# Query and key pieces of a head pair side by side in the attention operands: half as many operand transfers, each twice as large, and the row of maxima sent in two transfers

## The chip, the cores and the metric

The kernel runs on one core of one Trainium2 chip. The metric is the device time of one execution in microseconds (us); lower is better. The timeline positions used below are microseconds from the start of the profiled span.

## The reference, cut to what matters

Two sequences of 512 tokens with 128 features pass through four conditioned layers: a gated recurrent layer with ternary weights, a transformer block with 16 heads (no mask), a masked block of MLPs, and a causal transformer block with 16 heads. The change touches only the two attentions. For layer 3 the reference is

```
qkv = (x @ Wqkv).reshape(b, t, 3, H, hd).transpose(2, 0, 3, 1, 4)
scores = einsum('bhqd,bhkd->bhqk', q, k) * hd ** -0.5
scores = where(causal, scores, -inf)
attn = softmax(scores, axis=-1)
out = einsum('bhqk,bhkd->bhqd', attn, v)
```

with H = 16 heads of hd = 8 features. Layer 1 does the same without the causal mask.

## The kernel before, in words

**Operands.** Queries and keys are fp32 values that are split into three bf16 pieces each (high, middle, low; `spl`, held in the tile `tern`). A score is the sum of six products of pieces, so a head needs 8 features times 6 pieces; with a row of zeros and a row that carries the softmax maximum this makes 8 rows a feature and 64 rows a head. Two heads (a pair) stand above each other in the 128 partitions. These operands are the "stacks", in the tile `big`: partition 8i + place holds one piece of feature i, and along the row lie, for attention a, first all queries and then all keys: `p (a k b r t)`, with k = query or key, b = batch, r = head pair (8 of them), t = token (512). `stack_of` (L79) cuts out a head. `PIECES` and `PIECES_K` say which query and which key piece meet in each of the six products, `PLACE` at which of the 8 rows the product stands.

**Stack transfers.** The pieces are computed in feature layout and have to be spread to every eighth partition by DMA. The SP queue does this in L317 to L325: for each attention, for each batch b, for each part (high, middle, low, made by ScalarE at L1157, ScalarE at L1161 and VectorE at L835), for queries and then keys, it waits until that part of that operand is made and issues the transfers that need it. Each is 128 KB: 128 runs of 1 KB, from 128 partitions to 16 (`stacks[PLACE[j]::8, a, qk, b]`). There are 12 for each batch of each attention, 48 in all. TensorE waits for the 12 of batch 0 at L1488, before the first score product of the attention, and for those of batch 1 at L1460, half way through. The order of issue in batch 0 is three query transfers when the high query piece is there, three key transfers, two and two for the middle pieces, one and one for the low ones.

**Maxima.** A unit u is four heads of one batch; an attention has 8 units. In a unit TensorE computes the scores with queries as rows (L1469, in ring slots handed out by `schedule`, L243), VectorE takes the negated maximum over the keys (L961) into `nm`, GpSimd splits the 16 columns of `nm` into three bf16 parts (`max_parts`, L432 to L443, into `nm3`), TensorE turns `nm3` (L1437), VectorE copies the result to `nmp` (L966: 64 partitions by 128), and SP sends it (L326 to L331) in one transfer of 16 KB, 64 runs of 256 bytes, from 64 partitions into 8 partitions of `big`, the rows `MAX_PLACE` of the query stacks of the two head pairs of the unit. Then TensorE computes the scores a second time, now with keys as rows and the maximum inside the product (L1506); it waits for the maxima's row at L1501, once a unit. ScalarE takes the exponential (L1192), and TensorE multiplies by the values (L1483). All instructions of an engine run in the order in which they are written; TensorE's order is written out at L1510 to L1531.

**Fill.** Early on, three transfers (L313 to L315) put zeros and ones into the remaining rows of `big` from an array in DRAM, `in_fill`: one to 16 partitions at a step of 8 and two to 8 partitions at a step of 16, each with 64 KB for every partition.

Of the kernel before, what the change touches and what calls it, by code (L numbers as in the profile page):

```python
# [57 lines left out]
def build(nc, x_in, out, wa_in, w0_in, w1_in, w2_in, w3_in, row0_in, rowa_in, rowg_in, col_in, mask_in, c_in, ident_in,  # L58
          cmask_in, inv_in, sel_in, fill_in):
    with ExitStack() as ctx:  # L60
# [16 lines left out]
        stacks = big[:, :].rearrange("p (a k b r t) -> p a k b r t", a=2, k=2, b=B, r=NP)  # L77

        def stack_of(a, qk, b, h, lo, hi):  # L79

            row = 64 * (h % 2)
            return stacks[row:row + 64, a, qk, b, h // 2, lo:hi]
# [81 lines left out]
        spl = tern[:, 0:6 * B * S].rearrange("p (k i b t) -> p k i b t", k=2, i=3, b=B)  # L164
        resid = tern[:, 6 * B * S:6 * B * S + 4 * S].bitcast(F32).rearrange("p (k t) -> p k t", k=2)
# [4 lines left out]
        nm3 = sb("nm3", [128, 2, 2, MPARTS, 8], BF16)  # L170
# [115 lines left out]
        def _(sp):  # L286
# [30 lines left out]
            for a, (layer, causal) in enumerate(((1, False), (3, True))):  # L317

                for b in range(B):
                    for part, made in enumerate(("hi", "mid", "split")):  # L320
                        for qk, pieces in enumerate((PIECES, PIECES_K)):
                            sp.wait_ge(sem(f"a{a}_{made}"), 2 * b + qk + 1)
                            for j in [j for j, piece in enumerate(pieces) if piece == part]:
                                sp.dma_start(stacks[PLACE[j]::8, a, qk, b], spl[:, qk, part, b, :]).then_inc(  # L324
                                    sem(f"a{a}_stack{b}"), 16)  # L325
                for u in range(2 * TB):  # L326
                    b, g = u // 4, u % 4

                    sp.wait_ge(sem(f"a{a}_nmp"), u + 1)
                    sp.dma_start(stacks[MAX_PLACE::16, a, 0, b, 2 * g:2 * g + 2], nmp[:, u % 2]).then_inc(  # L330
                        sem(f"a{a}_mrow{u % 2}"), 16)  # L331
# [7 lines left out]
        def _(pool):  # L339
# [76 lines left out]
            for n, kind, layer in SEQ:  # L416
# [11 lines left out]
                if kind == "att":  # L428
# [3 lines left out]
                    def max_parts(u):  # L432

                        m = nm[:, u % 2].rearrange("p (k r) -> p k r", k=2)
                        pool.wait_ge(sem(f"a{a}_max"), n_max * (u + 1))
                        part = [nm3[:, u % 2, :, i] for i in range(3)]
                        left = nmr[:].rearrange("p (k r) -> p k r", k=2)
                        link(nc.gpsimd.tensor_copy(part[0], m))  # L438
                        link(nc.gpsimd.tensor_tensor(left, m, part[0], ALU.subtract))
                        link(nc.gpsimd.tensor_copy(part[1], left))  # L440
                        nc.gpsimd.tensor_tensor(part[2], left, part[1],
                                                ALU.subtract).then_inc(sem(f"a{a}_nm3"), 1)
                        pool.wait_ge(sem(f"a{a}_nm3"), u + 1)  # L443
# [38 lines left out]
        def _(dve):  # L482
# [443 lines left out]
            for n, kind, layer in SEQ:  # L926
                if kind == "att":
# [6 lines left out]
                    for item, u, *step_ in (x for slot in schedule(len(steps)) for x in slot):  # L934
# [20 lines left out]
                        if item == "max":  # L955
# [3 lines left out]
                            first = 8 * (hs[0] % 2) + TB * (hs[0] // 2) + qt  # L959
                            dst = nm[:, u % 2, first:first + TB * (len(hs) - 1) + 1:TB]  # L960
                            v.tensor_reduce(dst, src[:, 0:w * len(hs)].rearrange("p (h w) -> p h w", w=w),  # L961
                                            AX.X, ALU.max, negate=True).then_inc(sem(f"a{a}_max"), 1)
                        elif item == "parts":
                            if u >= 2:
                                dve.wait_ge(sem(f"a{a}_mrow{u % 2}"), 16 * (u // 2))
# [246 lines left out]
        def _(pe):  # L1212
# [185 lines left out]
            for n, kind, layer in SEQ:  # L1398
                if kind == "att":
# [22 lines left out]
                    def ring_item(item, u, i=0):  # L1422
# [33 lines left out]
                        else:  # L1456
                            qt, hs, wd = steps[i]
                            if u == 4 and i == 0:
                                pe.wait_ge(sem(f"a{a}_split"), 4)
                                pe.wait_ge(sem(f"a{a}_stack1"), 16 * 2 * len(PIECES))  # L1460
# [27 lines left out]
                    pe.wait_ge(sem(f"a{a}_stack0"), 16 * 2 * len(PIECES))  # L1488
# [6 lines left out]
                    def scores(s):  # L1495
# [4 lines left out]
                        if kt == 0 and p == 0:  # L1500
                            pe.wait_ge(sem(f"a{a}_mrow{u % 2}"), 16 * (u // 2 + 1))  # L1501
# [121 lines left out]
```

## Time and profile before

| | us |
|---|---|
| median of 3 runs (lowest to highest) | 458.74 (458.56 to 458.84) |
| the profiled execution | 458.03 |
| its span (first to last instruction) | 456.3 |
| TensorE matmul busy in the span | 303.2 (66%) |
| VectorE busy | 307.5 (67%) |
| ScalarE busy | 240.1 (53%) |
| GpSimd busy | 133.7 (29%) |
| DMA queue of SP, share of the 16 DMA engines | 13.7% |
| attention of layer 1, first to last maximum and score | about 174 to 283 |
| attention of layer 3 | about 336 to 434 |

1.7 us of the execution lie outside the span. Engines work beside each other, so busy times don't add up; what sets the time is the chain of work that ended last, followed back from release to release. In the rows below, "idle before <-X" in square brackets is the time for which the engine had nothing to do and what ended it; SPq is the instruction queue of the SP engine, which issues the DMAs; PEld is TensorE's load of the stationary operand. The granted TensorE clock is 1.00 for 2.4 GHz and 0.50 for 1.2 GHz.

### The profile page before, as it was taken

The numbers are of one execution on the slowest core, as the hardware profiler recorded it, in microseconds if no ns is written. First come the engines' busy times: TensorE is split into PE (matmuls) and PEld (weight loads), VectorE is DVE, ScalarE is ACT, GpSimd is POOL, SyncE is SP. The second block draws the span as 40 slices with busy tenths as digits, with TensorE's granted clock in tenths as the row PEclk, the third lists the DMA queues.
The fourth block names the chain that finished last, engine by engine and source line by source line (L and its number), as shares of the span: only waits on it lengthen the run. The fifth ranks groups of instructions, "written<-read, shape, count | busy, mean of one in ns | idle before, by whom it ended". The sixth has DMA issues, their size and how long they took to land.

```text
span 456.3 us, 5838 instructions
## 1 busy us (share of the span) xinstructions
PE 303.2 (66%) x1953; PEld 148.0 (32%) x1954; DVE 307.5 (67%) x791; ACT 240.1 (53%) x422; POOL 133.7 (29%) x237
## 2 busy tenths in 40 slices
PE   0012862642055647699999987885777899889686
PEld 0001821431022432122222222554443444344254
DVE  0688788776858865999999950433568678766330
ACT  2276926555166421267777777433342456665742
POOL 0013102232236240253223004218340344444520
PEclk9999985555555576679999999999796599999999
DMA  7960044000000033200000000000037000000001
GB/s 240 414 260 0 1 92 94 0 0 0 0 1 1 0 96 102 79 5 1 3 3 2 3 2 1 0 1 0 0 84 195 3 5 2 3 3 5 2 0 46
DMA packets 12138, 19.96 MB, mean 44 GB/s; under 512 B 2598, under 2 KB 11050, under 8 KB 11434
## 3 DMA queue, kind: packets, MB, share of 16 engines
q1 hardware_dynamic: 12108, 19.59, 13.7%
q8 instruction: 15, 0.25, 0.2%
q14 instruction: 15, 0.12, 0.1%
HBM read 12.51 MB, written 0.52 MB: 29 GB/s over the span
## 4 chain that ended last, share of the span: by engine, by line
PE 38%; DVE 30%; ACT 11%; POOL 7%; issue 6%; DMA 3%; SPq 2%; DVEq 0%; ACTq 0%; POOLq 0%
DVE nm L961 10%; PE ps L1483 8%; PE ps L1469 6%; PE pe L1395 4%; PE ps L1551 4%; PE pe L1506 3%; POOL rstd L344 2%; PE ps L1442 2%; ACT scr L1079 2%; DMA big<-nmp 2%; DVE st L539 2%; SPq L324 1%; DMA big<-in_wa 1%; DVE xn L549 1%; PE ps L1266 1%
## 5 line engine op out<-in xcount | busy, mean ns | idle before, releaser
L961 DVE TENSOR_REDUCE nm<-ps 128x1 f32<-128x512 f32 (+2 forms) x224 | 131.8, 647 | 21.6 <-PE ps L1469 20.4
L1192 ACT ACTIVATE scr<-pe 128x1024 f32<-128x1024 f32 (+3 forms) x128 | 105.6, 867 | 66.0 <-PE pe L1506 65.0
L1469 PE MATMUL ps<-big 64*128 64x512 bf16 (+3 forms) x256 | 71.4, 381 | 6.9 <-DVE nm L961 4.5
L1483 PE MATMUL ps<-scr 128*32 128x512 f32 (+3 forms) x512 | 58.8, 531 | 6.3 <-ACT scr L1167 4.8
L344 POOL TENSOR_TENSOR rstd<-var,half 128x4 f32<-128x4 f32 x26 | 28.5, 1097 | 102.7 <-DVE var L544 77.2
L1506 PE MATMUL pe<-big 64*128 64x512 bf16 (+3 forms) x256 | 44.0, 355 | 3.4 <-ACT scr L1192 2.0
L1469 PEld LDWEIGHTS ps<-big 64*128 64x128 bf16 x256 | 21.0, 101 | 54.1 <-DVE nm L961 44.3
L450 POOL TENSOR_SCALAR_AFFINE_SELECT scr<-scr 128x256 f32<-128x256 f32 x64 | 25.8, 407 | 37.7 <-ACT scr L1192 36.4
L438 POOL CAST nm<-nm 128x16 bf16<-128x16 f32 x16 | 3.1, 196 | 87.2 <-DVE nm L961 87.2
L1466 PE MATMUL ps<-cmask 64*128 64x128 bf16 (+1 forms) x192 | 25.7, 261 | 3.3 <-DMA big<-tern 2.8
L549 DVE TENSOR_SCALAR xn<-x_tok,mv,rstd 128x128 f32<-128x128 f32 x60 | 17.1, 348 | 15.8 <-POOL rstd L344 15.8
L1395 PE MATMUL pe<-hT,w 128*128 128x512 f32 x48 | 24.5, 635 | 3.5 <-ACT hT L1146 3.5
L1205 ACT ACTIVATE scr<-pe,col 128x512 f32<-128x512 f32 x24 | 16.3, 688 | 14.5 <-PE pe L1395 14.5
L1506 PEld LDWEIGHTS pe<-big 64*128 64x128 bf16 x256 | 12.8, 94 | 33.6 <-ACT scr L1192 18.8
L990 DVE TENSOR_TENSOR x_tok<-x_tok,ps 128x512 f32<-128x512 f32 x6 | 4.1, 687 | 21.3 <-PE ps L1551 21.2
L1071 ACT ACTIVATE junk<-scr 128x128 f32<-128x128 f32 x24 | 7.1, 297 | 21.0 <-DVE scr L672 20.9
L1266 PE MATMUL pe<-ident,xn 128*128 128x128 f32 x20 | 4.4, 358 | 20.6 <-ACT xn L1079 13.0
L1483 PEld LDWEIGHTS ps<-scr 128*32 128x32 f32 x512 | 10.4, 108 | 21.4 <-issue 10.2
L1079 ACT ACTIVATE scr<-scr,magic,q 128x128 f32<-128x128 f32 x32 | 12.7, 480 | 8.2 <-DVE q L693 8.2
L1146 ACT ACTIVATE hT<-ps,modc 128x512 f32<-128x512 f32 x8 | 6.2, 776 | 20.3 <-PE ps L1266 20.3
L1266 PE MATMUL ps<-ident,scr 128*128 128x128 f32 x24 | 6.4, 431 | 15.2 <-ACT scr L1079 14.4
L976 DVE RECIPROCAL rec<-ps 128x16 f32<-128x16 f32 x16 | 4.0, 252 | 18.5 <-PE ps L1442 18.5
(222 smaller groups left out, 584.1 us busy)
## 6 DMA issues: line engine op xcount, KB each, us to landing
big<-tern SPq DMA_DIRECT2D x48, 128.0 KB, 2.4
big<-in_wa SPq DMA_DIRECT2D x1, 2304.0 KB, 12.7
w<-in_w SPq DMA_DIRECT2D x2, 1152.0 KB, 19.5
big<-in_wa SPq DMA_DIRECT2D x1, 1344.0 KB, 6.4
big<-in_w SPq DMA_DIRECT2D x1, 1024.0 KB, 14.6
w<-in_w SPq DMA_DIRECT2D x1, 896.0 KB, 20.2
rowg<-in_rowg SPq DMA_DIRECT2D x1, 832.0 KB, 18.6
row<-in_row SPq DMA_DIRECT2D x1, 640.0 KB, 14.8
```

Of the source, the lines that this page charges most:

```text
L344: nc.gpsimd.tensor_tensor(dst, src, half[0:src.shape[0], 0:n], ALU.pow).then_inc(sem(done), 1)
L450: nc.gpsimd.affine_select(block_, block_, [[0, 2], [1, 128]], ALU.is_ge, 0.0, base=0, channel_multiplier=-1).then_inc(sem(f"a{a}_low"), 1)
L549: last = v.tensor_scalar(xn[:, t], x_tok[:, t], mv[:, t, 0:1], rstd[:, t:t + 1], ALU.subtract, ALU.mult)
L961: v.tensor_reduce(dst, src[:, 0:w * len(hs)].rearrange("p (h w) -> p h w", w=w), AX.X, ALU.max, negate=True).then_inc(sem(f"a{a}_max"), 1)
L1079: last = s_.activation(dst[:, t], src[:, t], ACT.Identity, bias=magic[:, 0:1], scale=q4[:, 3, m, t:t + 1])
L1192: s_.activation(P[:, kt % 2, 2 * p:2 * p + 2, q0:S], E[(e - 1) % 2][:, :, q0:S], ACT.Exp, scale=SCALE).then_inc(sem(f"a{a}_p"), 1)
L1395: t_.matmul(bank[2 + i % 4], m["w"][:, m["at"] + c * D:m["at"] + (c + 1) * D], hT[:, b], start=True, stop=True).then_inc(sem(f"n{n}_h"), 1)
L1466: t_.matmul(diagonal, cmask[row:row + 64, m], above.broadcast_to([64, len(hs), 128]), start=(m == 0), stop=False, skip_group_check=True)
L1469: last = t_.matmul(dst[:, k * wd:(k + 1) * wd], stack_of(a, 0, b, HG * g + h, qt * 128, (qt + 1) * 128), stack_of(a, 1, b, HG * g + h, 0, ...
L1483: last = t_.matmul(bank[6][32 * h:32 * h + 32, q0:S], V[b][:, kt, HG * g + h, :], P[:, kt % 2, h, q0:S], start=(kt == 0), stop=(kt == TB - 1),
L1506: last = t_.matmul(E[s % 2][:, j, q0:S], stack_of(a, 1, b, h, kt * 128, (kt + 1) * 128), stack_of(a, 0, b, h, q0, S), start=True, stop=True)
L1551: last = t_.matmul(bank[6 + b][:, i * D:(i + 1) * D], hid[:, b, c, i * D:(i + 1) * D], gated_w(n, b, c), start=(c == 0), stop=(c == m["n"] ...
```

## The change

In the stacks the query and the key of a head pair now lie side by side: `p (a b r k t)`. For one product j, the query piece and the key piece go to the same 16 partitions, and in them to neighbouring rows of 512 tokens, so one transfer of 256 KB carries both. Its source has for each of 128 partitions two runs of 1 KB that are a fixed step apart. It can be issued when the later of the two pieces is made, for both operands: the SP queue now waits for query and key together (`2 * b + 2`). Of the six transfers of a batch, one (j = 0) goes out after the high pieces, three (j = 1, 3, 4) after the middle pieces, two (j = 2, 5) after the low ones. TensorE's waits count 6 transfers in place of 12. The query rows of the two head pairs of a unit no longer lie next to each other, so the maxima's row is sent in two transfers of 8 KB, from 32 partitions each, and the waits for it count 32 in place of 16; `nm` and `nm3` are ordered by head pair first to fit. The filling array has its ones where the keys now lie.

```diff
@@ -74,12 +74,12 @@
 
         big = sb("big", [128, 2 * NH * B * S], BF16)
         QK_N = NP * B * S
-        stacks = big[:, :].rearrange("p (a k b r t) -> p a k b r t", a=2, k=2, b=B, r=NP)
+        stacks = big[:, :].rearrange("p (a b r k t) -> p a b r k t", a=2, k=2, b=B, r=NP)
 
         def stack_of(a, qk, b, h, lo, hi):
 
             row = 64 * (h % 2)
-            return stacks[row:row + 64, a, qk, b, h // 2, lo:hi]
+            return stacks[row:row + 64, a, b, h // 2, qk, lo:hi]
         wf32 = big[:, :].bitcast(F32)
         NWA, NW0 = sum(WA_N), sum(W0_N)
         wa_f = wf32[:, 0:NWA]
@@ -162,12 +162,13 @@
 
 
         spl = tern[:, 0:6 * B * S].rearrange("p (k i b t) -> p k i b t", k=2, i=3, b=B)
+        spl_ = tern[:, 0:6 * B * S].rearrange("p (k b t) -> p k b t", k=6, b=B)
         resid = tern[:, 6 * B * S:6 * B * S + 4 * S].bitcast(F32).rearrange("p (k t) -> p k t", k=2)
         V = [scr[:, 4096 + 2048 * b:6144 + 2048 * b].rearrange("p (t h e) -> p t h e", t=TB, h=NH) for b in range(B)]
         P = scr[:, 0:2 * HG * S].rearrange("p (i h t) -> p i h t", i=2, h=HG)
         hid = scr[:, 0:4 * 2 * S].rearrange("p (b c t) -> p b c t", b=B, c=4)
         nm = sb("nm", [128, 2, 16])
-        nm3 = sb("nm3", [128, 2, 2, MPARTS, 8], BF16)
+        nm3 = sb("nm3", [128, 2, 4, MPARTS, 4], BF16)
         nmr = sb("nmr", [128, 16])
         nmp = sb("nmp", [64, 2, 128], BF16)
         oT = scr[:, 8192:9216].rearrange("p (k t) -> p k t", k=2)
@@ -318,17 +319,18 @@
 
                 for b in range(B):
                     for part, made in enumerate(("hi", "mid", "split")):
-                        for qk, pieces in enumerate((PIECES, PIECES_K)):
-                            sp.wait_ge(sem(f"a{a}_{made}"), 2 * b + qk + 1)
-                            for j in [j for j, piece in enumerate(pieces) if piece == part]:
-                                sp.dma_start(stacks[PLACE[j]::8, a, qk, b], spl[:, qk, part, b, :]).then_inc(
-                                    sem(f"a{a}_stack{b}"), 16)
+                        sp.wait_ge(sem(f"a{a}_{made}"), 2 * b + 2)
+                        for j in [j for j in range(6) if max(PIECES[j], PIECES_K[j]) == part]:
+                            q_piece, k_piece = PIECES[j], 3 + PIECES_K[j]
+                            both = spl_[:, q_piece:k_piece + 1:k_piece - q_piece, b]
+                            sp.dma_start(stacks[PLACE[j]::8, a, b], both).then_inc(sem(f"a{a}_stack{b}"), 16)
                 for u in range(2 * TB):
                     b, g = u // 4, u % 4
 
                     sp.wait_ge(sem(f"a{a}_nmp"), u + 1)
-                    sp.dma_start(stacks[MAX_PLACE::16, a, 0, b, 2 * g:2 * g + 2], nmp[:, u % 2]).then_inc(
-                        sem(f"a{a}_mrow{u % 2}"), 16)
+                    for pair in range(2):
+                        sp.dma_start(stacks[MAX_PLACE::16, a, b, 2 * g + pair, 0],
+                                     nmp[32 * pair:32 * pair + 32, u % 2]).then_inc(sem(f"a{a}_mrow{u % 2}"), 16)
             for b in range(B):
                 sp.wait_ge(sem("x_done"), b + 1)
                 sp.dma_start(out[b].rearrange("(t p) d -> p t d", p=128), x_tok[:, bt(b)]).then_inc(sem("stored"), 16)
@@ -431,10 +433,10 @@
 
                     def max_parts(u):
 
-                        m = nm[:, u % 2].rearrange("p (k r) -> p k r", k=2)
+                        m = nm[:, u % 2].rearrange("p (k r) -> p k r", k=4)
                         pool.wait_ge(sem(f"a{a}_max"), n_max * (u + 1))
                         part = [nm3[:, u % 2, :, i] for i in range(3)]
-                        left = nmr[:].rearrange("p (k r) -> p k r", k=2)
+                        left = nmr[:].rearrange("p (k r) -> p k r", k=4)
                         link(nc.gpsimd.tensor_copy(part[0], m))
                         link(nc.gpsimd.tensor_tensor(left, m, part[0], ALU.subtract))
                         link(nc.gpsimd.tensor_copy(part[1], left))
@@ -956,13 +958,13 @@
                             qt, hs, w = steps[step_[0]]
                             if u >= 2 and step_[0] == 0:
                                 dve.wait_ge(sem(f"a{a}_nm3"), u - 1)
-                            first = 8 * (hs[0] % 2) + TB * (hs[0] // 2) + qt
-                            dst = nm[:, u % 2, first:first + TB * (len(hs) - 1) + 1:TB]
+                            first = 8 * (hs[0] // 2) + TB * (hs[0] % 2) + qt
+                            dst = nm[:, u % 2, first:first + 8 * (len(hs) - 1) + 1:8]
                             v.tensor_reduce(dst, src[:, 0:w * len(hs)].rearrange("p (h w) -> p h w", w=w),
                                             AX.X, ALU.max, negate=True).then_inc(sem(f"a{a}_max"), 1)
                         elif item == "parts":
                             if u >= 2:
-                                dve.wait_ge(sem(f"a{a}_mrow{u % 2}"), 16 * (u // 2))
+                                dve.wait_ge(sem(f"a{a}_mrow{u % 2}"), 32 * (u // 2))
                             v.tensor_copy(nmp[:, u % 2], src.bitcast(BF16)[0:64, 0:128]).then_inc(sem(f"a{a}_nmp"), 1)
                         elif item == "proj":
                             dve.wait_ge(sem("n_bias"), B * n + u + 1)
@@ -1457,7 +1459,7 @@
                             qt, hs, wd = steps[i]
                             if u == 4 and i == 0:
                                 pe.wait_ge(sem(f"a{a}_split"), 4)
-                                pe.wait_ge(sem(f"a{a}_stack1"), 16 * 2 * len(PIECES))
+                                pe.wait_ge(sem(f"a{a}_stack1"), 16 * len(PIECES))
                             if causal:
                                 diagonal = dst[:, 0:wd * len(hs)].rearrange("p (h w) -> p h w", w=wd)[:, :, wd - 128:wd]
                                 row = 64 * (hs[0] % 2)
@@ -1485,7 +1487,7 @@
                                              tile_position=(0, 32 * h))
                         last.then_inc(sem(f"a{a}_pv"), 1)
 
-                    pe.wait_ge(sem(f"a{a}_stack0"), 16 * 2 * len(PIECES))
+                    pe.wait_ge(sem(f"a{a}_stack0"), 16 * len(PIECES))
                     pe.wait_ge(sem("filled"), 16 * 3)
                     pe.wait_ge(sem("n_var"), B * n + 2)
                     for x in slots[0]:
@@ -1498,7 +1500,7 @@
                         b, g = u // 4, u % 4
                         q0 = 128 * kt if causal else 0
                         if kt == 0 and p == 0:
-                            pe.wait_ge(sem(f"a{a}_mrow{u % 2}"), 16 * (u // 2 + 1))
+                            pe.wait_ge(sem(f"a{a}_mrow{u % 2}"), 32 * (u // 2 + 1))
                         if s >= 2:
                             pe.wait_ge(sem(f"a{a}_p"), s - 1)
                         for j in range(2):
@@ -1609,7 +1611,7 @@
         "col": np.stack(cols, 1), "mask": g["mask_BxS_bk0"].reshape(B * TB, 128).T, "c": g["cond_1024"],
         "ident": np.eye(128, dtype=np.float32), "cmask": cmask.astype(ml_dtypes.bfloat16),
         "inv": np.tile(np.array([1.0 / k for k in numel], np.float32), (128, 1)), "sel": sel,
-        "fill": np.stack([np.zeros(2 * NH * B * S), np.tile(np.repeat([0.0, 1.0], NP * B * S), 2)]).astype(ml_dtypes.bfloat16),
+        "fill": np.stack([np.zeros(2 * NH * B * S), np.tile(np.repeat([0.0, 1.0], S), 2 * NP * B)]).astype(ml_dtypes.bfloat16),
     }
     arrays = {k: np.ascontiguousarray(v) for k, v in arrays.items()}
     nc = bacc.Bacc("TRN2", target_bir_lowering=False, num_devices=1)
```

## Rows read from the trace of the kernel before

**Rows 1.** The page, chain that ended last: share of the span by line

```profile
DVE nm L961 10%; PE ps L1483 8%; PE ps L1469 6%; PE pe L1395 4%; PE ps L1551 4%; PE pe L1506 3%; POOL rstd L344 2%; PE ps L1442 2%; ACT scr L1079 2%; DMA big<-nmp 2%; DVE st L539 2%; SPq L324 1%; DMA big<-in_wa 1%; DVE xn L549 1%; PE ps L1266 1%
```

**Rows 2.** Chain in order of time, around 340: start us, us, what

```profile
336.37 0.55 SPq L324
...
343.42 2.37 DMA big<-tern
...
345.83 0.62 PE ps L1466 x4
```

**Rows 3.** Timeline of layer 3's start: start, us, engine, line, op, tiles, [idle before]

```profile
338.19 1.22 ACT L1161 CAST tern<-tern 128x512 bf16<-128x512 f32 x2 [0.99 <-DVE tern L831]
338.84 1.29 DVE L835 TENSOR_TENSOR tern<-tern 128x512 bf16<-128x512 f32 x2
...
345.83 0.14 PEld L1466 LDWEIGHTS ps<-cmask 64*128 64x128 bf16 x4 [3.01 <-DMA big<-tern]
...
345.95 0.68 DVE L847 COPY scr<-pe 128x512 f32<-128x512 f32 x1
...
346.69 5.97 DVE L961 TENSOR_REDUCE nm<-ps 128x2 f32<-128x256 f32 x11
```

**Rows 4.** Lines L324 and L330: issue time ns (min/median/max), and landing

```profile
L324 SPq DMA_DIRECT2D big<-tern x48: 531/600/615, 164.4 to 351.2; - x48
...
DMA to landing us min/median/max: 2.3/2.4/2.6
...
L330 SPq DMA_DIRECT2D big<-nmp x16: 579/590/629, 193.4 to 419.7; - x16
```

**Rows 5.** Windows: stretch, length, five engines' busy us, PEclk, DMA share, GB/s

```profile
65.00:69.80 4.80, 2.04 (x4) 0.37 (x2) 4.63 (x9) 3.74 (x19) 1.00 (x1) 0.59 1.01 218
69.80:74.70 4.90, 0.36 (x2) 0.40 (x3) 3.79 (x11) 3.54 (x8) 1.75 (x2) 0.50 0.50 107
...
11.00:16.00 5.00, 0.56 (x2) 0.50 (x2) 1.81 (x10) 2.08 (x6) 0.00 (x0) 1.00 0.98 419
337.60:345.40 7.80, 3.53 (x16) 2.15 (x16) 5.10 (x9) 4.34 (x8) 1.27 (x1) 1.00 0.74 202
```

**Rows 6.** Timeline of layer 1's start

```profile
166.28 0.62 ACT L1161 CAST tern<-tern 128x512 bf16<-128x512 f32 x1 [0.24 <-DVE tern L831]
...
174.24 0.10 PEld L1469 LDWEIGHTS ps<-big 64*128 64x128 bf16 x1 [0.33 <-DMA big<-tern]
...
174.35 0.78 ACT L1146 ACTIVATE hT<-pe,modc 128x512 f32<-128x512 f32 x1 [7.46 <-PE pe L1266]
```

**Rows 7.** Timeline and chain: issue of maxima's rows, and the scores that wait for them

```profile
193.36 0.61 SPq L330 DMA_DIRECT2D big<-nmp  x1
...
195.35 1.36 PE L1506 MATMUL pe<-big 64*128 64x512 bf16 x4
...
355.09 0.63 SPq L330 DMA_DIRECT2D big<-nmp  x1
...
357.04 0.65 PE L1506 MATMUL pe<-big 64*128 64x512 bf16 x2
...
203.29 0.61 SPq L330 DMA_DIRECT2D big<-nmp  x1
...
205.67 0.10 PEld L1506 LDWEIGHTS pe<-big 64*128 64x128 bf16 x2
...
213.69 0.58 SPq L330 DMA_DIRECT2D big<-nmp  x1
...
216.67 0.10 PEld L1506 LDWEIGHTS pe<-big 64*128 64x128 bf16 x2
...
235.69 3.61 DMA big<-nmp
```

**Rows 8.** Windows of the low clock in layer 3, and TensorE's timeline at its end

```profile
345.80:362.80 17.00, 15.65 (x97) 7.57 (x97) 14.08 (x27) 4.57 (x6) 2.68 (x11) 0.50 0.32 89
...
360.95 1.93 PE L1483 MATMUL ps<-scr 128*32 128x512 f32 x8
```

## The prediction, made before any run of the changed kernel

> **What bounds the kernel now.** I read the chain that ended last first. No engine owns it: the maxima on VectorE have a tenth of the span, the products with the values 8%, and of what the change touches only two small entries appear, the stack issues on SP's queue (1%) and the maxima's transfers (2%) [rows 1]. So the change can act at few places. Next the chain in order of time. At layer 3's start it runs along SP's queue: the first stack transfer is issued at 336.37, the twelfth at 343.42, 0.64 us apart, and TensorE starts 2.4 us after the last, at 345.83 [rows 2]. The timeline shows TensorE idle for 3.0 us there, ended by the transfer; but VectorE, which must take the first maximum next, is busy with other work until 346.63 and starts at 346.69 [rows 3]. So the stacks are late for TensorE, and only just in time for VectorE: earlier stacks gain little, later ones cost in full. At layer 1's start TensorE waits 0.33 us only [rows 6]. Last, the maxima's rows: 16 issues of 0.59 us, a time that a stack issue of eight times the bytes has too [rows 4].
>
> **The transfers: what an issue and 256 KB take.** An issue takes 0.60 us whether it carries 64 runs or 128 [rows 4], so I take 0.64 from issue to issue for the new ones too; the upper bound is double, one issue that takes the time of the two it replaces, 1.29 us. What the bytes take is the question. The stack stream now moves 202 GB/s with the DMA engines busy for 0.74 of the time [rows 5]: filled up, that would be 202 / 0.74 = 273 GB/s and 0.96 us for 256 KB. Nearer is the fill of the very same partitions (16 at a step of 8), which keeps all 16 engines busy (share 1.01) and still moves 218 GB/s, and with 8 partitions on half the engines 107; loads to all 128 partitions reach 419 at the same share [rows 5]. I read this as the destination being the limit: engines that write to these 16 partitions get in each other's way. Then 256 KB take 262144 B / 218 GB/s = 1.2 us. The bounds are 0.64 (issue alone) and 1.29. I take 1.2, since it is the saturated row with the same destination, and back-to-back transfers of 256 KB with 0.64 between issues will saturate.
>
> The Trainium skill has two rules that pull apart here. "DMA: Bandwidth & Descriptors", in its rules for kernel authors, says to coalesce many small transfers into a large one; by its line of bytes over 436 GB/s, 256 KB would take 0.6 us (an estimate from that page), and the sum would be that of the fast rival below. "SBUF — State Buffer", in the section on the DMA port swizzle, says that a partition's port is set by bits 2 to 4 and bit 6 of its number, by which 16 partitions at a step of 8 reach only half of the 16 ports. The fill's 218 against 419 GB/s sides with the second.
>
> **Layer 3, batch 0.** Before, half of the transfers (the query pieces and first key pieces) went out from 336.37 on, while later pieces were being made. Now five of six wait for the middle key piece, ready at 338.19 + 1.22 = 339.41 [rows 3]; the first is long through by then. The low pieces are there at 338.84 + 1.29 = 340.13 [rows 3] and are not late, since three transfers stand before them. The fixed part of a transfer is 2.4 - 0.64 = 1.75 us [rows 4]. So the last lands at 339.45 + 1.75 + 5 x 1.2 = 347.2, against 345.8: TensorE starts 1.4 us later, VectorE with it: **+1.4**. Bounds: with 0.64 it lands at 344.4, 1.4 earlier, of which VectorE, free at 345.95 + 0.68 = 346.63 only, would pass on little, so -1.4 is the end and -0.1 the likely value there; with 1.29, 347.65, +1.9. Batch 1's six transfers queue behind and end about 354.5, before the first maxima's row of this attention is issued at 355.09 [rows 7], which is itself pushed back: 0.
>
> **Layer 1, batch 0.** The middle key piece is ready at 166.28 + 0.62 = 166.90 [rows 6]: 166.95 + 1.75 + 6.0 = 174.7. Before, twelve issues from 164.4 on gave 164.4 + 11 x 0.64 + 2.4 = 173.9 [rows 4]. TensorE comes to the wait at about 174.2, makes one maximum's scores in 0.6 us and then needs the modulated input of batch 1, ready at 174.35 + 0.78 = 175.13 [rows 6]: **+0.1**, bounds 0 and +0.6. Batch 1 is not wanted for a long time: 0.
>
> **The maxima's rows.** The second transfer of each unit is issued 0.64 us after the first, so the row is complete up to 0.64 us later; its bytes are nothing. VectorE's copy waits only for the row two units back. Who waits is TensorE at L1501, and behind it every later score and ring item. The unit's time from issue to scores tells the slack, since a row lands within 1.95 us (355.09 to 357.04 [rows 7]). The first units of both attentions have 1.99 and 1.95 us [rows 7]: nothing to spare beyond what hides behind running matmuls; **+0.4** and **+0.5** (each 0 to 0.65). The second unit has 2.38 [rows 7], in both attentions: **+0.1** each at most, 0.1 together. The later ones have 2.98 as in 213.69 to 216.67 [rows 7], which covers 1.95 + 0.64: 0. That holds for nine of the twelve remaining units; in the other three the transfer itself was slow, as the 3.61 at 235.69 [rows 7], and TensorE waited for it. A transfer issued 0.64 us later on the same stalled engine probably ends with the first: **+0.2** for the three, bounds 0 and 1.9.
>
> **The rest.** GpSimd's four small operations and VectorE's maxima write the same number of elements at another step; the fill moves the same bytes; neither is timed otherwise: 0. SP issues 24 fewer stack transfers and 16 more maxima's transfers, and nobody waits for its queue elsewhere.
>
> **The clock.** TensorE runs at 1.2 GHz from about 345.8 to 362.8 in layer 3, and at the end of that stretch the chain is TensorE's: eight value products take 1.93 us there [rows 8]. If the rise stays at its place, the 1.9 us of work that is pushed past it runs at twice the speed: up to -0.95. I take **-0.7**. If the rise moves with the work or beyond it, nothing is given back and more is lost.
>
> **Sum.** 1.4 + 0.1 + 0.4 + 0.5 + 0.1 + 0.2 - 0.7 = +2.0 us. On the profiled execution that is 458.03 + 2.0 = 460.0; the median of the runs, 458.74, is 0.7 above it, so I forecast **460.7** for the median.
>
> **Rivals.**
> (a) *The port limit is milder* (0.96 us for 256 KB, the engines' own rate): the stacks land at 346.0, +0.2, and the sum is 0.2 + 1.2 - 0.4 = +1.0 or less; with a first-unit delay that hides behind VectorE, +0.6: 459.4. For it: the stream's 0.74 share. Against: the fill. Chance 0.22.
> (b) *Faster*: transfers are paced by issue alone (0.64). The stacks are there at 344.4, before the clock falls, between 345.4 [rows 5] and 345.8 [rows 8]. Then TensorE has work earlier and the clock can stay up in the 17 us [rows 8]. From 357.04 [rows 7] to 362.8 the chain is mostly TensorE's, 5.8 us at the low clock, half of it at the other: -0.1 - 2.9 + 1.0 (maxima's rows, a little cheaper so) = -2.0, 456.7. It decides at the stacks' landing: before about 345. For it: the wait of 3.0 us is real. Against: the fill's rate. Chance 0.12.
> (c) *The clock rises later*: the late start leaves one stretch emptier, the low clock lasts some 3 us longer, and instead of -0.7 it costs about +1.5: 462.9. Chance 0.2.
> (d) *An issue of 256 runs takes twice as long* (1.29): five issues end the chain at 339.45 + 4 x 1.29 + 2.4 = 347.0 or a little more, nearly my number by another cause: 460.7. It would show in the issue rows. Chance 0.05.
> My forecast has the remaining 0.41.
>
> **How the numbers follow.** A measurement of this kernel tells a change of 0.2% (0.9 us) from none. Faster by more than that is (b), with a part of (a)'s low end: 0.13. Within: most of (a) and the low end of the forecast: 0.24. Slower: 0.63. The range takes in (a), (c) and the bounds of the maxima's rows, and leaves out (b) and the largest sums: 458.0 to 463.3.
>
> **What would show it.** In the changed profile the stack transfers should have issues of about 0.6 us but land, the last of batch 0, 4 to 5 us after issue instead of 2.4; a window over them should show about 215 GB/s with a DMA share near 1; TensorE's wait at layer 3's start should grow from 3.0 to about 4.4 us and VectorE's first maximum come 1.3 us later against its L847 copy. The maxima's row should show two issues 0.64 us apart and a wait of TensorE at the first unit of each attention, and none in the third. I am wrong if the landing stays at 2.4 to 3 us, or if the stacks arrive before 345.8.

## The result and the profile after

The changed kernel took **465.84 us** (median of 4 runs, 465.80 to 466.63) against 458.78 for the kernel before (4 runs beside it): a ratio of 1.0136 with an interval of 1.0094 to 1.0178, 7.06 us more. I forecast 460.7 with a range of 458.0 to 463.3: slower was right, the size was not. Run again on another chip (after_again) it stood at 1.0113 (1.0087 to 1.0139), 5.2 us more at 460, with the kernel before between 458.65 and 461.63 in 15 executions. The two intervals overlap; I take 5.2 us, which rests on more executions, for the change's average. The profile below is one execution, and its 7.8 us also depend on where the steps of TensorE's clock fell in it.

| | before | after |
|---|---|---|
| profiled execution, us | 458.03 | 465.80 |
| span, us | 456.3 | 464.0 |
| matmul busy, us | 303.2 | 309.6 |
| VectorE busy, us | 307.5 | 307.5 |
| DMA queue of SP, share of 16 engines | 13.7% | 15.2% |

VectorE did the same work in the same time; matmuls took 6.4 us more with the same count of 1953. The page after, chain that ended last, answers to [rows 1]:

```profile
PE 38%; DVE 31%; ACT 10%; POOL 8%; issue 6%; DMA 5%; SPq 2%; DVEq 0%; POOLq 0%; ACTq 0%
DVE nm L963 12%; PE ps L1485 8%; PE ps L1471 5%; PE ps L1553 4%; PE pe L1397 4%; DMA big<-tern 3%; PE pe L1508 3%; POOL rstd L346 2%; PE ps L1444 2%; ACT scr L1081 2%; DVE st L541 2%; PE ps L1268 1%; DVE xn L551 1%; DMA big<-in_wa 1%; PE pe L1234 1%
...
big<-tern SPq DMA_DIRECT2D x24, 256.0 KB, 4.8
```

The stack transfers are now 3% of the chain by themselves, and their median from issue to landing is 4.8 us where it was 2.4 [rows 4]. The chain in order of time at layer 3's start, which answers to [rows 2]:

```profile
343.98 0.60 SPq L326
344.62 0.61 SPq L326
345.27 0.62 SPq L326
345.94 0.62 SPq L326
346.60 5.92 DMA big<-tern
352.57 0.62 PE ps L1468 x4
```

Issues are still 0.6 us, but the last transfer lands 5.9 us after its issue, because those ahead of it are still moving. A window over the stream (columns as in [rows 5]):

```profile
345.50:352.00 6.50, 3.73 (x11) 2.15 (x9) 3.07 (x5) 3.40 (x5) 0.00 (x0) 0.74 1.11 216
```

216 GB/s with a DMA share above 1: the engines are full, at the rate of the fill, 218 GB/s [rows 5], and not at that of a load to all partitions.

From the products that make queries and keys (339.14 in the timeline after, 334.60 before) to TensorE's start on the stacks it is 13.43 us, before 11.23: 2.2 us more. In layer 1 the stacks land at 175.17, 1.2 us later than before. TensorE then makes the products of batch 1 at 1.2 GHz:

```profile
175.21 0.60 PE L1471 MATMUL ps<-big 64*128 64x512 bf16 x1 [1.07 <-DMA big<-tern]
175.75 2.07 PE L1362 MATMUL ps<-hT,w 128*128 128x512 f32 x2
177.75 0.61 PE L1471 MATMUL ps<-big 64*128 64x512 bf16 x2
178.29 2.07 PE L1362 MATMUL pe<-hT,w 128*128 128x512 f32 x2
```

The second pair (the key product) took 1.48 us before, at 2.4 GHz from 178.5 on; now 2.07, since the clock rises at 181.6 only. The copy of unit 0's maxima, 193.12 before, starts at 194.85. Then the maxima's row of that unit, in the chain of the changed kernel (answers to [rows 7]):

```profile
194.93 0.14 DVE nmp L968
195.07 0.02 issue
195.08 0.65 SPq L332
195.73 0.04 issue
195.77 2.21 DMA big<-nmp
197.99 0.14 issue
198.12 0.58 PE pe L1508
```

3.04 us from issue to scores against 1.99 [rows 7]. A larger item stands behind it. Windows of the changed kernel, then of the kernel before, over 198.9 to 205.5:

```profile
198.90:205.50 6.60, 6.24 (x28) 1.33 (x24) 4.51 (x8) 4.15 (x5) 1.86 (x5) 0.50 0.01 2
205.50:212.10 6.60, 6.13 (x43) 1.43 (x42) 6.26 (x12) 5.26 (x6) 2.38 (x4) 1.00 0.01 2
```

```profile
198.90:205.50 6.60, 6.16 (x45) 1.38 (x42) 6.19 (x12) 5.35 (x6) 4.23 (x8) 1.00 0.01 2
```

For 6.6 us TensorE is at 1.2 GHz where it was at 2.4, and gets 28 matmuls done in place of 45. From the first exponential of unit 0 to that of unit 1 it is 11.55 us against 9.99. Whether the change moved this rise, or only this execution has it there, the two profiles can't tell; the experiments come back to it.

### The profile page after: what moved, and what is told of

Its sections match the earlier page's. It is cut to its first block, busy times and chain, and to the rows that moved or that the text cites. A ratio compares the mean times of both kernels' runs of the same rounds, so it can differ in the third digit from the quotient of the medians.

```text
span 464.0 us, 5830 instructions
## 1 busy us (share of the span) xinstructions
PE 309.6 (67%) x1953; PEld 150.6 (32%) x1954; DVE 307.5 (66%) x791; ACT 240.2 (52%) x422; POOL 133.8 (29%) x237
## 3 DMA queue, kind: packets, MB, share of 16 engines
q1 hardware_dynamic: 11852, 19.59, 15.2%
## 4 chain that ended last, share of the span: by engine, by line
PE 38%; DVE 31%; ACT 10%; POOL 8%; issue 6%; DMA 5%; SPq 2%; DVEq 0%; POOLq 0%; ACTq 0%
DVE nm L963 12%; PE ps L1485 8%; PE ps L1471 5%; PE ps L1553 4%; PE pe L1397 4%; DMA big<-tern 3%; PE pe L1508 3%; POOL rstd L346 2%; PE ps L1444 2%; ACT scr L1081 2%; DVE st L541 2%; PE ps L1268 1%; DVE xn L551 1%; DMA big<-in_wa 1%; PE pe L1234 1%
## 5 line engine op out<-in xcount | busy, mean ns | idle before, releaser
L1485 PE MATMUL ps<-scr 128*32 128x512 f32 (+3 forms) x512 | 59.8, 539 | 6.3 <-ACT scr L1169 4.8
L1397 PE MATMUL pe<-hT,w 128*128 128x512 f32 x48 | 24.8, 641 | 3.5 <-ACT hT L1148 3.5
L1207 ACT ACTIVATE scr<-pe,col 128x512 f32<-128x512 f32 x24 | 16.3, 688 | 15.2 <-PE pe L1397 15.2
```

The source lines that it names most:

```text
L1397: t_.matmul(bank[2 + i % 4], m["w"][:, m["at"] + c * D:m["at"] + (c + 1) * D], hT[:, b], start=True, stop=True).then_inc(sem(f"n{n}_h"), 1)
L1485: last = t_.matmul(bank[6][32 * h:32 * h + 32, q0:S], V[b][:, kt, HG * g + h, :], P[:, kt % 2, h, q0:S], start=(kt == 0), stop=(kt == TB - 1),
```

## The experiments

Two theories stood against each other first: the stacks' lateness with the clock (1), or the second maxima transfer (2); and whether the lateness comes from deferral or from the size of the transfers (3). The clock's steps fall at other places in each execution, so a profile shows a delay directly, and the ratios, from many executions, the average.

### Two maxima transfers alone (maxrow_two)

```diff
-                    sp.dma_start(stacks[MAX_PLACE::16, a, 0, b, 2 * g:2 * g + 2], nmp[:, u % 2]).then_inc(
-                        sem(f"a{a}_mrow{u % 2}"), 16)
+                    for pair in range(2):
+                        sp.dma_start(stacks[MAX_PLACE::16, a, 0, b, 2 * g + pair],
+                                     nmp[32 * pair:32 * pair + 32, u % 2]).then_inc(sem(f"a{a}_mrow{u % 2}"), 16)
...
```

Left out of the cut are the order of `nm` and `nm3` and the waits for 32, as in the change.

> The kernel before, with only the maxima's row sent in two transfers (and nm, nm3 ordered by head pair); stacks as before. Theory 1 (the stacks' lateness is the cause, the clock's rise doubles it): the scores of the first unit of each attention come 0.5 to 0.7 us later, the other units not at all; without a moved clock step that is +1.0 to +1.3 us, 459.8 to 460.0; if the clock's rise in layer 1 moves too, one step of about 3.4 us later costs up to 1.6 more. Theory 2 (the second maxima transfer is the main cost): most of the 7 us is here, 464 or more.

Ratio 1.0057 (1.0032 to 1.0082), 2.6 us (1.5 to 3.8): twice my price, and half of the change's average. The profile bears out the places: from unit 0's copy to the first exponential it is 0.70 us longer in layer 1 (3.90 against 3.20) and 0.56 in layer 3 (3.44 against 2.88). In its chain the second issue follows at once, and its transfer lands 2.20 us behind it:

```profile
194.19 0.64 SPq L331
194.84 0.04 issue
194.88 2.20 DMA big<-nmp
197.08 0.14 issue
197.22 1.01 PE pe L1507 x3
```

The other 1.3 us of the 2.6 aren't in these two waits, and where they lie on average stays open. In this profile unit 0 to unit 1 takes 11.55 us, with the clock low until 203.8, as in the changed kernel. Layer 3 loses another 1.5 us: its first maximum comes 13.59 us behind the products that make queries and keys (12.09 before), though the stacks are as early (11.34 and 11.23). The products of batch 1 fell into a low stretch there:

```profile
343.68 2.04 PE L1361 MATMUL ps<-hT,w 128*128 128x512 f32 x2 [1.87 <-ACT hT L1147]
```

The same pair took 1.13 us in the kernel before. early_halves, below, has the two maxima transfers too and doesn't lose this (11.96).

### The new layout with the old transfers (early_halves)

```diff
+                        for qk, pieces in enumerate((PIECES, PIECES_K)):
+                            sp.wait_ge(sem(f"a{a}_{made}"), 2 * b + qk + 1)
+                            for j in [j for j, piece in enumerate(pieces) if piece == part]:
+                                sp.dma_start(stacks[PLACE[j]::8, a, b, :, qk], spl[:, qk, part, b, :]).then_inc(
+                                    sem(f"a{a}_stack{b}"), 16)
```

> The changed kernel's layout and its two maxima transfers, but twelve stack transfers of 128 KB a batch in the order and at the waits of the kernel before (each operand goes as soon as its own piece is made). Theory 1: the layout costs nothing, so this is maxrow_two's time within 0.5 us, and TensorE starts layer 3 about 3 us after its idle began, as before. Rival (the layout itself, 2 KB steps between the runs in a destination row, slows the writes): each transfer lands later than 2.4 us and the time is 1 us or more above maxrow_two's.

Ratio 1.0041 (1.0018 to 1.0065), not to be told from maxrow_two. From product to TensorE's start in layer 3 it is 11.28 us (11.23 before, 11.34 in maxrow_two), and landings are as before:

```profile
L325 SPq DMA_DIRECT2D big<-tern x48: 531/600/617, 164.6 to 354.4; - x48
...
DMA to landing us min/median/max: 2.3/2.4/2.6
```

No cost of the layout shows, in the time or in a landing.

### The changed kernel's order in halves (late_halves), and in the kernel before (before_late)

```diff
+                        sp.wait_ge(sem(f"a{a}_{made}"), 2 * b + 2)
+                        for j in [j for j in range(6) if max(PIECES[j], PIECES_K[j]) == part]:
+                            for qk, piece in enumerate((PIECES[j], PIECES_K[j])):
+                                sp.dma_start(stacks[PLACE[j]::8, a, b, :, qk], spl[:, qk, piece, b, :]).then_inc(
+                                    sem(f"a{a}_stack{b}"), 16)
```

> The changed kernel, but each 256 KB transfer split into its query and its key half of 128 KB; waits and order of products as in the changed kernel. Theory 1a (deferral: ten of twelve half transfers have to follow the middle key piece, whatever their size): the last lands 9 x 0.64 + 2.4 = 8.2 us after the middle key piece, against 8.5 in the changed kernel, so about the changed kernel's time, 465.3 to 466. Theory 3 (the transfer of 256 KB itself is slow, by its size or shape): the landing is clearly earlier, and 1.5 us or more of the 7 come back.

Ratio 1.0122 (1.0084 to 1.0161), with the changed kernel's 1.0113 inside. Product to TensorE's start is 13.08 us, against 13.43 with whole transfers and 11.25 or so with early halves. So about 1.8 us of the 2.2 come from waiting for both operands, and 0.35 or less from the transfers' size (two further profiles with whole transfers, after_again and probe, have 13.39 and 13.13).

Layer 1 shows the same, ahead of its clock's rise. From the start of the last middle key piece (the second CAST at L1161, in the changed kernel L1163) to the first product of batch 1, TensorE takes 8.90 or 8.91 us in before, early_halves, maxrow_two and mixed, 9.37 and 9.38 in before_late and late_halves, and 9.65, 9.34 and 9.35 in after, after_again and probe: 0.45 us for deferral, up to 0.75 with whole transfers.

The run before_late makes the same edit in the kernel before (`stacks[PLACE[j]::8, a, qk, b]`), with one maxima transfer:

> The kernel before (its layout, one maxima transfer, twelve stack transfers of 128 KB a batch), with the stack transfers at the waits and in the order of the changed kernel: both operands of a product behind the later piece. Theory 1: deferral alone is the larger part. The parts should add: late_halves (deferral and two maxima transfers) stood at 1.0122 and maxrow_two (two maxima transfers alone) at 1.0057, so 1.005 to 1.009 here, with the last stack transfer of layer 3's batch 0 landing about 2 us later after the first piece than before. Rival: the parts don't add, since either alone moves the clock's rise; then 1.009 or more.

Ratio 1.0057 (1.0031 to 1.0082), with the wait itself as expected, 13.03 us. Its chain (the longest pieces alone) shows the issues behind the middle key piece, and a last transfer that lands as fast as ever:

```profile
340.69 1.23 ACT tern L1161 x2
...
343.14 0.61 SPq L324
...
345.09 0.61 SPq L324
345.74 0.61 SPq L324
...
347.68 2.39 DMA big<-tern
350.12 0.62 PE ps L1466 x4
```

The parts add, as far as intervals of 0.25% each can tell: 0.57% for deferral and 0.57% for the maxima's rows, against 1.13% for the change.

### What limits a stream of transfers (probe)

Behind the last store of the changed kernel stand four streams of eight transfers, with one wait at each stream's end:

```diff
+            both = spl_[:, 0:4:3, 0]
+            for i in range(8):
+                sp.dma_start(stacks[PLACE[i % 6]::8, i // 6, 0], both).then_inc(sem("stored"), 16)
...
+            for i in range(8):
+                sp.dma_start(big[i % 4::4, 4096 * (i // 4):4096 * (i // 4) + 4096], both).then_inc(sem("stored"), 16)
...
+            for i in range(8):
+                sp.dma_start(big[:, 1024 * i:1024 * i + 1024], both).then_inc(sem("stored"), 16)
...
+            for i in range(8):
+                sp.dma_start(stacks[PLACE[i % 6]::8, 0, 1, :, i // 6], spl[:, 0, 0, 0, :]).then_inc(sem("stored"), 16)
```

> The changed kernel, with four streams of transfers added behind the last store, each of 8 transfers issued without a wait between them, so that the time is longer by some 50 us. a: 256 KB to 16 partitions at a step of 8, as the stacks; b: the same source and bytes to 32 partitions at a step of 4; c: the same to all 128 partitions; d: 128 KB to 16 partitions at a step of 8. Theory of destination ports: a needs 1.2 to 1.35 us per transfer (about 200 to 218 GB/s), b and c are paced by the issue or the engines at 0.64 to 0.8 us (330 to 410 GB/s), d by its issue at 0.64. Rival (runs of 1 KB or SBUF to SBUF copies are the limit): a, b and c take the same, 1.2 us or more.

The windows of the four streams in order, a to d:

```profile
462.00:471.60 9.60, 0.00 (x0) 0.00 (x0) 0.00 (x0) 0.00 (x0) 0.00 (x0) 0.50 1.05 217
473.60:479.90 6.30, 0.00 (x0) 0.00 (x0) 0.00 (x0) 0.00 (x0) 0.00 (x0) 0.50 0.97 323
481.50:487.70 6.20, 0.00 (x0) 0.00 (x0) 0.00 (x0) 0.00 (x0) 0.00 (x0) 0.50 0.98 325
489.30:494.60 5.30, 0.00 (x0) 0.00 (x0) 0.00 (x0) 0.00 (x0) 0.00 (x0) 0.50 0.69 186
```

Stream a: eight transfers in 9.6 us, 1.2 us each. The same source and bytes go to 32 partitions at a step of 4 or to all 128 in 0.79 and 0.78 us each, with the engines nearly as full. So it is the destination that holds the rate at two thirds (217 against 323 and 325 GB/s), not the runs of 1 KB nor the copy inside SBUF, and 1.2 us for 256 KB was right. Whether it is which partitions or how few of them, no stream separates: none goes to 16 partitions that lie otherwise. Stream d is bound by its issue: 5.3 us for eight, 0.66 each. That is why merging two transfers could save little here: 1.2 us for the bytes replace two issues of 0.64. By the port rule of the Trainium skill ("SBUF — State Buffer", the DMA port swizzle) stream a reaches 8 of 16 ports, b and c all 16; the streams agree in direction, though b and c gain a factor of 1.5 and not 2, and for these transfers I go by the measured factor.

### The mix (mixed)

The changed kernel with 256 KB only where both pieces are made together, j = 0 and j = 4, and 128 KB for the rest as soon as made, ten transfers a batch:

```diff
...
+                    sp.wait_ge(sem(f"a{a}_hi"), 2 * b + 1)
+                    halves(1, 0)
+                    halves(2, 0)
+                    sp.wait_ge(sem(f"a{a}_hi"), 2 * b + 2)
+                    whole(0)
+                    halves(3, 1)
+                    halves(5, 1)
+                    sp.wait_ge(sem(f"a{a}_mid"), 2 * b + 2)
+                    halves(3, 0)
+                    halves(1, 1)
+                    whole(4)
+                    sp.wait_ge(sem(f"a{a}_split"), 2 * b + 2)
+                    halves(2, 1)
+                    halves(5, 0)
```

`whole(j)` issues the 256 KB of product j, `halves(j, qk)` the 128 KB of its query (0) or key (1).

> The changed layout and two maxima transfers, with ten stack transfers a batch: 256 KB where both pieces are made together (j = 0, j = 4), 128 KB for the eight other halves, each issued as soon as its piece is made. If deferral is the cause (theory 1), the last transfer of layer 3's batch 0 lands at or up to 1 us before where it did in the kernel before, and the time is that of early_halves or less, 459 to 462. If transfers of 256 KB are harmful by themselves, it is above early_halves.

Ratio 1.0061 (1.0038 to 1.0084). Product to TensorE's start in layer 3 falls to 10.97 us, 0.26 less than in the kernel before, and TensorE waits 0.9 us for the last transfer where it waited about 3:

```profile
L324 SPq DMA_DIRECT2D big<-tern x32: 536/605/632, 164.4 to 353.2; - x32
...
  PEld ps L1487: 1.0, 1
  PE ps L1487: 0.9, 1
```

The time is that of the two maxima transfers alone (1.0057). Earlier stacks bring nothing here: VectorE takes layer 3's first maximum 13.59 us behind the products, busy until then with batch 1, and does so in maxrow_two as well.

### The changed kernel once more, and added matmuls (after_again, after_busy, before_busy, before_busy3)

> The changed kernel once more, on the chip on which the kernels beside it run. The kernel before, unchanged, took 458.0 to 462.4 us on another chip, with the steps of TensorE's clock at other places from execution to execution; so the 7.06 us may hold a share that belongs to one placement of these steps. Theory 1: against the kernel before the median is 5 to 7 us longer here too. If the 7.06 us were mostly placement, it is 3 us or less.

Ratio 1.0113 (1.0087 to 1.0139), 5.2 us: at the low end of what theory 1 expected. How much of the first 7.06 us was the place of the clock's steps, these runs don't tell.

The added matmuls feed nothing; they write a bank that is overwritten before it is read:

```diff
+                    for _ in range(0 if a else 24):
+                        t_.matmul(bank[RING[0]], cmask[:, 0], cmask[:, 0:4].rearrange("p k t -> p (k t)"),
+                                  start=True, stop=True)
                     attention_turn(n, 1)
...
+                    for _ in range(13 if a else 0):
+                        t_.matmul(bank[RING[0]], cmask[:, 0], cmask[:, 0:4].rearrange("p k t -> p (k t)"),
+                                  start=True, stop=True)
                     pe.wait_ge(sem(f"a{a}_stack0"), 16 * len(PIECES))
```

> The changed kernel, with added matmuls that feed nothing where TensorE waits: 24 of 512 columns ahead of the turn of batch 1 in layer 1, 13 ahead of the wait for the stacks in layer 3. The stacks land no earlier. Clock theory: the 1.2 GHz stretches at the two attention starts become shorter, and the time falls by 2 us or more against after_again. Rival (TensorE's clock is not what the late stacks cost): same time or up to 1 us more.

A miss: 1.0121 (1.0080 to 1.0162). In its profile the clock falls only at 174.9 in layer 1 (167.9 in the changed kernel), but the low stretch before the first scores still ends at 205.7, and unit 0 to unit 1 is 11.54 us.

> The kernel before, with the same kind of added matmuls: 24 ahead of the turn of batch 1 in layer 1, 11 ahead of the wait for the stacks in layer 3. Clock theory: it gains as well, 2 to 4 us, and is faster than both kernels. Rival: no gain.

Ratio 0.9974 (0.9948 to 1.0000), 1.2 us at the middle, less than expected and at the edge of what can be told.

> The kernel before with only the 11 added matmuls of 512 columns ahead of the wait for the stacks in layer 3. In before_busy the low clock of layer 3 began later and ended earlier, while in layer 1 the 24 did not help. If the layer 3 part carries the gain of before_busy (0.9974), this is 0.995 to 0.998; otherwise 1.000.

With 11 matmuls in layer 3 alone: 0.9985 (0.9951 to 1.0019), no difference that shows. In before_busy's profile the clock holds at layer 3's start until 351.5, 14.6 us behind the products, where it fell at 345.7, 11.1 us behind them, before:

```profile
345.80:351.40 5.60, 4.57 (x36) 2.18 (x35) 4.92 (x10) 2.10 (x3) 0.00 (x0) 1.00 0.75 204
351.60:361.60 10.00, 8.76 (x58) 4.73 (x56) 8.22 (x17) 1.95 (x3) 1.25 (x5) 0.50 0.30 82
```

before_busy3 has the instructions of the kernel before in layer 1, and there its clock rises at 204.9, against 198.9 in the profile of before. Its key product takes 2.08 us, as in the changed kernel, and it needs 11.34 us from unit 0 to unit 1. The other way round, probe is the changed kernel up to its last store, and in its profile the clock rises at 201.7. Two rows from before_busy3, and behind the dots one from probe:

```profile
178.28 2.08 PE L1360 MATMUL pe<-hT,w 128*128 128x512 f32 x2
198.90:204.80 5.90, 5.90 (x25) 1.15 (x24) 4.60 (x9) 3.69 (x5) 2.26 (x6) 0.50 0.00 0
...
201.80:205.50 3.70, 3.46 (x28) 0.74 (x25) 3.69 (x7) 3.54 (x4) 1.71 (x5) 1.00 0.00 0
```

| profile | rise in layer 1, us | unit 0 to unit 1, us |
|---|---|---|
| before | 198.9 | 9.99 |
| probe (changed kernel) | 201.7 | 10.17 |
| before_busy3 (layer 1 as before) | 204.9 | 11.34 |
| after | 205.5 | 11.55 |

So the place of this rise differs among executions of the same work, and with it what unit 1 costs, in either kernel. How often it falls where is on record for profiled executions alone.

### Matmuls between the maxima (after_warm, before_warm)

```diff
-                    for x in slots[0]:
+                    for k, x in enumerate(slots[0]):
                         ring_item(*x)
+                        if k > 8:
+                            t_.matmul(bank[TURN_BANK][:, 0:256], cmask[:, 0],
+                                      cmask[:, 0:2].rearrange("p k t -> p (k t)"), start=True, stop=True)
```

> after_busy, and one added matmul of 256 columns behind each ring item from the ninth on in the filling of the first two units of both attentions, where VectorE's maxima set the pace and TensorE ran at 1.2 GHz from 185 to 206 us in layer 1. after_busy did not shorten that stretch. Clock theory: with this one it ends by 195, the exponentials of unit 1 of layer 1 follow the copy of unit 0's maxima by 13 us or less in place of 15.5, and the time is 2 us or more below after_again's ratio of 1.0113 to the kernel before. Rival: the low stretch does not matter, since VectorE sets the pace; then it stays at 1.011 or more.

> The kernel before with the same added matmuls (24 and 11 at the waits, one of 256 columns behind each ring item from the ninth on). Clock theory: faster than before_busy, whose ratio to the kernel before was 0.9974; 0.993 to 0.996. Rival: as before_busy or worse, since the added matmuls delay VectorE's maxima while the clock is low.

Both much slower: 1.0223 (1.0185 to 1.0261) and 1.0239 (1.0211 to 1.0268). The clock rose no earlier for it, at 205.6 and 206.1. TensorE of before_warm was busy for 8.49 and 9.64 of two times 10 us and stayed at the low level (but for the first 0.6 us):

```profile
185.00:195.00 10.00, 8.49 (x21) 2.17 (x21) 8.70 (x15) 1.69 (x3) 3.28 (x9) 0.53 0.22 61
195.00:205.00 10.00, 9.64 (x34) 2.25 (x33) 7.78 (x12) 3.75 (x4) 1.81 (x2) 0.50 0.01 2
```

VectorE, 9.91 us busy in the first of these stretches in the kernel before, has 8.70 here: the added matmuls took TensorE's time at the low clock and held up the maxima. What makes the clock rise in this stretch stays open; these runs refute that added matmuls of this kind do.

## Why the prediction was wrong in size and right in sign

**256 KB in 1.2 us: right.** Stream a of the probe shows 1.2 us, and the changed kernel's stream 216 GB/s. The rivals with a milder limit (a) and with issue pacing (b) fall, and (d) with them, since an issue of a 256 KB transfer still takes 0.62 us at the median. TensorE's wait grew from 3.0 to 3.5 us only (4.4 forecast), since its work ahead of the wait ran into the low clock.

**Layer 3, batch 0, forecast +1.4: mis-sized, +2.2.** I took the fixed part of a transfer as 2.4 - 0.64 = 1.75 us. A 256 KB transfer alone (j = 0) lands 3.1 us after its issue, near the 2.95 that this gives; the first of the five, 2.2 us behind it, lands after 3.4. From there the pace is (352.52 - 347.4) / 4 = 1.3 us a transfer and not 1.2. Both together are the 0.8 us. The mechanism, deferral, was right: before_late and late_halves have 1.8 us of it with small transfers.

**Layer 1, batch 0, forecast +0.1: mis-sized, +0.45 to +0.75.** The stacks landed at 175.17, not 174.7, and TensorE started 1.0 us later. I had set the landing against the modulated input of batch 1 and not counted that half a microsecond more would make the stacks the later of the two. The rest of the profiled delay, 1.7 us at unit 0's copy, is the clock's rise at 181.6 in place of 178.5; in before_busy3, with the kernel before's instructions, the same stretch from the first product of batch 1 to that copy takes 18.8 us (17.9 before, 19.1 after), with the rise at 181.0.

**Maxima's rows, forecast 1.2: right in the waits, average too small.** The first units cost 0.7 and 0.56 us directly (0.4 and 0.5 forecast), 1.26 together. The third unit and later ones have their 2.98 us from issue to scores as before, with two issues inside:

```profile
217.70 1.21 SPq L332 DMA_DIRECT2D big<-nmp  x2
...
220.68 0.10 PEld L1508 LDWEIGHTS pe<-big 64*128 64x128 bf16 x2
```

The three slow transfers of before were not slow after. At unit 4 of layer 1 that gave nothing for good, since the kernel before had caught up at unit 5; at unit 5 of layer 3 it gave back 0.57 us. By many executions the part costs 2.6 us (1.5 to 3.8), so up to half lies outside the waits, and no run shows where.

**The clock, forecast -0.7: the step that failed.** I assumed that the rise at 362.8 stays while work is pushed past it. It did not stay: in the changed kernel it came at 369.3, and in the ten other profiles without matmuls between the maxima it lies 24.8 to 30.3 us behind layer 3's products (28.2 before, 30.2 after), wherever these fall. I find nothing given back. The waits by themselves, 1.9 to 2.2 in layer 3, 0.45 to 0.75 in layer 1 and 1.26 for the maxima's rows, make 3.6 to 4.2 us, and the average is 4.0 to 6.4; with -0.7 they would make 2.9 to 3.5. The other part of the miss is the two mis-sized stack terms, about 1.2 us together.

In the profiled execution the clock took much more: 1.2 us ahead of unit 0's copy and 1.55 between units 0 and 1 in layer 1, where I had put no clock term at all, and about 1.4 behind the attention of layer 3, where the changed kernel's profile has a low stretch and that of before has none from 362.8 to 454.9:

```profile
434.20:437.60 3.40, 3.27 (x18) 1.75 (x18) 0.55 (x2) 1.73 (x3) 0.81 (x2) 0.50 0.02 5
```

But the same costs stand in a profile of the kernel before with no more than 11 matmuls added at layer 3's start (before_busy3: the rise of layer 1 at 204.9, and a low stretch from 426.7 to 433.5), so they are not shown to be the change's. Rival (c) had the rise going with the work; its +1.5 is neither borne out nor refuted, since what the clock costs on average stays open between nothing and 2.8 us.

The account of the profiled 7.8 us, as the delay against the kernel before: at the first exponential of layer 1 it is 2.45 (stacks and clock 1.7, maxima's row 0.7); at unit 1, 4.0 (the clock); at layer 3's products 4.5; at its first maximum 6.7 (stacks); at its first exponential 7.3 (maxima's row); from unit 5 on 6.3 (the slow transfer of before at that unit, and 0.4 us at unit 1); at the end 7.7 (the clock).

## What to carry to other kernels

A merged transfer can leave only when its last piece is made: before halving the number of issues, set the time at which each half was sent against the chain, not the number of issues. Look up where a transfer's destination partitions lie; to 16 partitions at a step of 8 a stream moved 217 GB/s here, against 323 to 32 partitions at a step of 4, so larger transfers won nothing. Price a delay ahead of a rise in TensorE's clock with the rise moving too. And before a clock step that differs between two profiles is put down to a change, look for it in other executions of the same work.

## What the runs showed that I had not expected

The same kernel's time spreads over nearly 6 us on one chip (before: 457.64 to 463.48 in 23 runs) while another chip gave 458.56 to 458.84 in 4; the rise of TensorE's clock in layer 1 differs among profiles of the same work (198.9 and 204.9). TensorE busy for 18.1 of 20 us (before_warm) did not raise the clock. No version of these beat the kernel before beyond doubt; before_busy, at 0.9974, came nearest.
